# Last stage of a mixture-of-experts kernel: 71 tiles without a look-ahead behind them, rows of a partition side by side, first choices fetched early

## What is computed

```python
logits = flat @ gate_W.T                      # 4096 tokens, 8 experts
probs = softmax(logits); top_v, top_i = top_k(probs, 2)
g = silu(einsum('td,edf->etf', flat, w1_e))   # d=128, f=512
u = einsum('td,edf->etf', flat, w3_e)
out_e = einsum('etf,efd->etd', g * u, w2_e)
routed = einsum('te,etd->td', gates, out_e)
...
return 0.5 * shared + 0.5 * routed
x = x + gb * that                             # gb: one row of 128 per batch
```

## Time and profile before

| | us |
|---|---|
| median of 3 runs | 2277.46 (2275.94 to 2278.57) |
| profiled execution, its own time | 2262.21 |
| profiled execution, its span | 2260.4 |
| mean granted clock of TensorE in it | 0.987 |

### The profile page before, as it was taken

One profiled execution on the slowest core, in us unless ns is written; L12 is line 12 of the kernel. 1 busy time (PEld: TensorE's weight loads), 2 busy tenths in 40 slices (PEclk: granted clock), 3 DMA queues, 4 the chain that ended last, 5 costly groups with the idle time before them and its releaser, 6 DMA issues. The chain is left out here.

```text
span 2260.4 us, 40689 instructions
## 1 busy us (share of the span) xinstructions
PE 2172.6 (96%) x10606; PEld 1381.5 (61%) x10607; DVE 1811.6 (80%) x4826; ACT 1248.2 (55%) x1690; POOL 1385.5 (61%) x751
## 2 busy tenths in 40 slices
PE   7989999999999999999999999999999999989995
PEld 4756756556556565665656656565565654449884
DVE  7788887888888888888888888888888887765555
ACT  2333344566666666666666666666666663434442
POOL 2212121777777787787877777787777776643331
PEclk9999999999999999999999999999999999999997
DMA  7050220000001000000100000010000000411114
GB/s 251 26 201 1 87 80 31 24 17 13 16 18 33 17 13 16 18 14 16 31 16 18 16 14 13 16 36 17 14 13 18 17 8 11 153 43 49 47 45 138
DMA packets 90664, 91.79 MB, mean 41 GB/s; under 512 B 22261, under 2 KB 75125, under 8 KB 90553
## 3 DMA queue, kind: packets, MB, share of 16 engines
q1 hardware_dynamic: 86232, 81.88, 11.7%
q0 software_dynamic: 4352, 8.99, 1.2%
HBM read 57.90 MB, written 36.86 MB: 42 GB/s over the span
## 5 line engine op out<-in xcount | busy, mean ns | idle before, releaser
L1661 ACT ACTIVATE big<-P 128x1024 f32<-128x1024 f32 x512 | 512.6, 1021 | 99.6 <-PE P L2044 82.0
L2058 PE MATMUL P<-big,V 128*64 128x512 f32 x2048 | 470.5, 600 | 1.0 <-ACT big L1667 1.0
L658 POOL TENSOR_TENSOR spair<-spair,big 128x1024 f32<-128x1024 f32 x192 | 457.4, 2382 | 16.0 <-DVE hp L818 1.3
L658 POOL TENSOR_TENSOR opair<-opair,big 128x1024 f32<-128x1024 f32 x192 | 457.6, 2384 | 15.0
L1048 DVE CUSTOM_DVE_ANT_0 big<-P,near 128x512 f32<-128x512 f32 x512 | 349.0, 682 | 110.2 <-PE P L2028 107.7
L2028 PE MATMUL P<-kq 96*128 96x512 f32 x1008 | 414.2, 432 | 2.7 <-DVE kq L1036 1.4
L2043 PE MATMUL P<-kq 97*128 97x512 f32 x1024 | 409.5, 400 | 2.4 <-DVE xs L824 2.1
L1051 DVE TENSOR_REDUCE mhalf<-P 128x1 f32<-128x512 f32 x512 | 349.3, 682 | 76.7 <-PE P L2028 65.8
L2044 PE MATMUL P<-kq 128*128 128x512 f32 x1024 | 407.0, 397 | 0.0
L2028 PEld LDWEIGHTS P<-kq 96*128 96x128 f32 x1008 | 180.8, 189 | 204.1 <-issue 103.6
L2058 PEld LDWEIGHTS P<-big,V 128*64 128x64 f32 x2048 | 135.6, 137 | 266.3 <-issue 263.7
(11 more groups left out here) (333 smaller groups left out, 3636.2 us busy)
## 6 DMA issues: line engine op xcount, KB each, us to landing
slots<-later SPq DMA_DIRECT2D x4, 4224.0 KB, 16.1
kq<-auxrows SPq DMA_DIRECT2D x64, 128.0 KB, 2.2
wqk<-wparts SPq DMA_DIRECT2D x124, 64.0 KB, 1.8
big<-in_wex SPq DMA_DIRECT2D x8, 768.0 KB, 12.1
xt<-slots SPq DMA_DIRECT2D x76, 66.0 KB, 1.8
near<-in_aux SPq DMA_DIRECT2D x64, 64.0 KB, 1.8
big<-yrows SPq DMA_DIRECT2D x8, 512.0 KB, 7.2
xs<-in_x SPq DMA_DIRECT2D x4, 512.0 KB, 4.1
```

The source lines that it names most:

```text
L658: pool.tensor_tensor(psum8[s][:, :], psum8[s][:, :], pfull[:, j % RING, :], ALU.add).then_inc(S["p_added"], 1)
L1661: act.activation(pfull[:, j, :], banks(2 * (j % 2)), ACT.Exp, scale=DH1 ** -0.5).then_inc(S["exp_done"], 1)
L2058: mm = pe.matmul(P[64 * i:64 * i + 64, 4, :], V1[:, j, s, :], half(pfull[:, j, :], i), start=(j == 0), stop=(j == T - 1))
```

## The change

The number of steps becomes NT = 71, which is the most that can be filled (64 full tiles and 7 for the rounding). The loop now covers steps 24 to 47 alone, and steps 48 to 70 are written out on each engine, without the work for tiles that don't exist. The rows are renumbered: token p*8+t of a batch's numbering stands where t*128+p stood, so that a partition's eight rows lie side by side in `yrows` and are moved as one piece of 4 KB. The fetch is split: the four c = 0 transfers are issued as soon as the scatters of all tiles before the last expert's have landed (a count that DVE now works out in four operations more and puts at the end of `blk_i`, so that `S["map"]` goes to 4), the four c = 1 transfers at the end. DVE multiplies and adds c = 0 of batches 0 to 2 by themselves, ahead of c = 1; batch 3 is done as before. That is 15 operations on 128x1024 in place of 12.

```diff
+NT = K1N * NTOK // 128 + E1 - 1
+LAST = NSTEP // GROUP - 1
-    m[:, M_TOK:M_TOK + T] = 128 * np.arange(T) + i[:, None]
+    m[:, M_TOK:M_TOK + T] = np.arange(T) + T * i[:, None]
...
+        out_of = lambda i: 16 * len(range(i, NT, YBUF))
...
-            sp.wait_ge(S["map"], 2)
+            sp.wait_ge(S["map"], 4)
...
-            with sp.Fori(0, NSTEP // GROUP) as r:
+            with sp.Fori(0, LAST) as r:
...
+            for k in range(LAST * GROUP + XBUF, NT):
+                block = sp.value_load(blk_i[0:1, 0, k:k + 1], min_val=0, max_val=E1 * REGION)
+                sp.wait_ge(E["t_turned"], k - XBUF + 1)
+                sp.wait_ge(E["t_idx"], k - XBUF + 1)
+                load_tile(k, block)
+
+            def load_y(b, c):
+                rows = yrows[c * NTOK + b * N:c * NTOK + (b + 1) * N, :].rearrange("(p t) d -> p (t d)", p=128)
+                sp.dma_start(big[:, 2 * b + c, :], rows).then_inc(E[f"m_z_in{b}" if c else f"m_y_in{b}"], 16)
+
+            uptos = [sp.value_load(blk_i[0:1, 0, NBLK - 1 - i:NBLK - i], min_val=16 * NTOK // 128 // YBUF, max_val=out_of(YBUF - 1 if i else 0)) for i in range(2)]
             for i in range(YBUF):
-                sp.wait_ge(E[f"t_out{i}"], 16 * NSTEP // YBUF)
-            sp.wait_ge(E["t_down"], NSTEP)
+                sp.wait_ge(E[f"t_out{i}"], uptos[i // (YBUF - 1)])
             for b in range(B):
-                for c in range(K1N):
-                    rows = yrows[c * NTOK + b * N:c * NTOK + (b + 1) * N, :].rearrange("(t p) d -> p t d", p=128)
-                    sp.dma_start(tok(big[:, 2 * b + c, :]), rows).then_inc(E[f"m_y_in{b}"], 16)
+                load_y(b, 0)
+            for i in range(YBUF):
+                sp.wait_ge(E[f"t_out{i}"], out_of(i))
+            sp.wait_ge(E["t_down"], NT)
+            for b in range(B):
+                load_y(b, 1)
...
-                dve.tensor_scalar(blk_i[:, 0, :], block, float(E1 * REGION), None, ALU.min).then_inc(S["map"], 1)
+                dve.tensor_scalar(blk_i[:, 0, 0:NBLK - 2], block[:, 0:NBLK - 2], float(E1 * REGION), None, ALU.min).then_inc(S["map"], 1)
+                begun_at = ks[:, 0:NT:YBUF]
+                fills = later[:, 0:len(range(0, NT, YBUF)), 0]
+                step(dve.tensor_scalar(fills, begun_at, tiles_e[:, 2, E1 - 2:E1 - 1], 16.0, ALU.is_lt, ALU.mult))
+                stepped()
+                step(dve.tensor_reduce(tiles_e[:, 1, 0:1], fills, AX.X, ALU.add))
+                stepped()
+                for i, most in enumerate((out_of(0), out_of(YBUF - 1))):
+                    dve.tensor_scalar(blk_i[:, 0, NBLK - 1 - i:NBLK - i], tiles_e[:, 1, 0:1], float(most), None, ALU.min).then_inc(S["map"], 1)
...
-            with dve.Fori(1, NSTEP // GROUP) as r:
+            with dve.Fori(1, LAST) as r:
...
+            for j in range(GROUP):
+                left = NT - LAST * GROUP - j
+                if left > 3:
+                    tile_low(LAST, 3 + j, same)
+                if left > 1:
+                    tile_gu(LAST, 1 + j, same)
+                if left > 0:
+                    tile_out(LAST, j, same)
+                if left > 2:
+                    tile_dest(LAST, 2 + j, same)
+
+            AHEAD = 3
+            dve.wait_ge(E["m_x_in"], 16 * B)
+            for b in range(AHEAD):
+                ya, xb = tok(big[:, 2 * b, :]), tok(xs[:, b, :])
+                dve.wait_ge(E[f"m_y_in{b}"], 16)
                 dve.tensor_tensor(ya, ya, over(modb[:, b, :], tens), ALU.mult).then_inc(E["m_scaled"], 1)
                 dve.wait_ge(E["m_scaled"], b + 1)
-                xb = tok(xs[:, b, :])
-                dve.tensor_tensor(xb, xb, ya, ALU.add).then_inc(E["m_done"], 1)
+                dve.tensor_tensor(xb, xb, ya, ALU.add).then_inc(E["m_sum"], 1)
+            for b in range(B):
+                ya, yb, xb = tok(big[:, 2 * b, :]), tok(big[:, 2 * b + 1, :]), tok(xs[:, b, :])
+                dve.wait_ge(E[f"m_z_in{b}"], 16)
+                if b < AHEAD:
+                    dve.wait_ge(E["m_sum"], b + 1)
+                else:
+                    dve.wait_ge(E[f"m_y_in{b}"], 16)
+                    dve.tensor_tensor(yb, yb, ya, ALU.add).then_inc(E["m_sum"], 1)
+                    dve.wait_ge(E["m_sum"], b + 1)
+                dve.tensor_tensor(yb, yb, over(modb[:, b, :], tens), ALU.mult).then_inc(E["m_scaled"], 1)
+                dve.wait_ge(E["m_scaled"], AHEAD + b + 1)
+                dve.tensor_tensor(xb, xb, yb, ALU.add).then_inc(E["m_done"], 1)
...
+            es = experts_of(LAST * GROUP, GROUP)
+            for j in range(GROUP):
+                left = NT - LAST * GROUP - j
+                if left > 3:
+                    tile_turn(LAST, 3 + j, same)
+                if left > 2:
+                    tile_up(LAST, 2 + j, same, es[2 + j])
+                if left > 0:
+                    tile_down(LAST, j, same, es[j])
+                if left > 1:
+                    tile_gu_turn(LAST, 1 + j, same)
```

More of the change, by code:

```diff
@@ L203, in network @@
              "c_kept": S["ydT_copied"], "t_gate": S["gates"], "t_idx": S["dests"], "t_gu": S["gu_done"], "t_gu_turned": S["yd_turned"], "t_guT": S["hT_dve"],
-             "t_down": S["downd_mm"], "t_y": S["ydT_copied"], "m_x_in": S["mod_in"],
+             "t_down": S["downd_mm"], "t_y": S["ydT_copied"], "m_x_in": S["mod_in"], **{f"m_z_in{b}": S[n] for b, n in enumerate(("q0_mm", "k0_mm", "q0_min", "k0_min"))},
              "m_sum": S["x1_done"], "m_scaled": S["x1_scaled"], "m_done": S["x_ready"], "m_out": S["next_mod"]}
@@ L379, in end_batch @@
             e.sem_inc(G["passed"], 1)
+        assert XBUF == YBUF
+        out_of = lambda i: 16 * len(range(i, NT, YBUF))
         block = ctx.enter_context(nc.Block())
@@ L600, in _ @@
             for i in range(XBUF):
-                sp.wait_ge(G[f"t_in{i}"], 16 * (NSTEP + XBUF) // XBUF)
+                sp.wait_ge(G[f"t_in{i}"], out_of(i))
         @block.gpsimd
@@ L780, in _ @@
             end_batch(pool, -1)
-            with pool.Fori(0, NSTEP // GROUP) as r:
+            with pool.Fori(0, LAST) as r:
                 for j in range(GROUP):
@@ L787, in _ @@
                     pool.indirect_dma_start(yrows, bass.IndirectOffsetOnAxis(tidx[:, j % YBUF:j % YBUF + 1], 0), xn[:, j % YBUF, :], None).then_inc(E[f"t_out{j % YBUF}"], 16)
+            for k in range(LAST * GROUP, NT):
+                pool.wait_ge(E["t_y"], k + 1)
+                pool.indirect_dma_start(yrows, bass.IndirectOffsetOnAxis(tidx[:, k % YBUF:k % YBUF + 1], 0), xn[:, k % YBUF, :], None).then_inc(E[f"t_out{k % YBUF}"], 16)
         @block.vector
@@ L1893, in _ @@
                 tile_guT(0, 1 + j, same)
-            with act.Fori(1, NSTEP // GROUP) as r:
+            with act.Fori(1, LAST) as r:
                 for j in range(GROUP):
@@ L1898, in _ @@
                     tile_guT(r, 1 + j, act.snap)
+            for j in range(GROUP):
+                left = NT - LAST * GROUP - j
+                if left > 3:
+                    tile_T(LAST, 3 + j, same)
+                if left > 2:
+                    tile_silu(LAST, 2 + j, same)
+                if left > 1:
+                    tile_guT(LAST, 1 + j, same)
         @block.tensor
@@ L2516, in _ @@
                 tile_gu_turn(0, 1 + j, same)
-            with pe.Fori(1, NSTEP // GROUP) as r:
+            with pe.Fori(1, LAST) as r:
                 es = experts_of(r * GROUP, GROUP + 4)
```

## The result

| | before | after |
|---|---|---|
| median, us | 2277.46 (7 runs, 2275.94 to 2279.53) | 2268.61 (7 runs, 2262.71 to 2271.38) |
| profiled execution, its own time | 2262.21 | 2270.38 |
| its span | 2260.4 | 2268.5 |

The ratio is 0.996, 95% interval [0.995, 0.9969]: 8.9 us faster, between 7.1 and 11.4. The forecast was 2267.8.

A forecast was written before the change was run, and what follows sets the result against it. PE was taken to bound the stage until 2233, then waiting and elementwise work. Gains of 4.2 + 0.5 - 0.4 + 5.4 = 9.7 us off 2277.46 gave 2267.8, range 2264 to 2273.

The forecast's parts named there:

- Drain: Last steps: tile 71 gone, then without look-ahead each step a chain of 2.20 us; gains 4.2 us, bounds 3.4 to 4.25.
- Border: PE loading experts' numbers at tile 48: nearest to the first border, 2.05 above pitch; 0.5 us gained, bounds 1.5 gained, 0.5 lost.
- Contention: Scatters beside the early fetch land in 6.0 us instead of 2.3, delaying tiles 69 and 70; 0.4 us lost, bounds 0 to 1.0.
- Tail: Last copy to DVE's end: six operations under the hand-over, nine after; 24.26 us becomes 18.9, 5.4 gained.
- The map: Four more DVE operations, about 1 us, covered by SP's wait for POOL's drain; cost nothing, 1 us if uncovered.
- The leeway: Time from a scatter's start until it must have landed for the indices four tiles on: 4.9 us.
- longer-contention rival: Scatters 64 to 67 all at 6.0 us or more, drained steps late too; 2.5 us lost beyond the 0.4, 2270.3; chance 0.12.
- The rival in which it is locked out: DVE's six operations delay POOL's last scatter to 7.75 us behind the last copy; gain only 3.8, 2273.7; chance 0.05.
- rivals of the numbering: Rows 4 KB apart make scatters land late throughout the stage; at 6.0 us, 40 us more, about 2308; chance 0.03.
- the fetch that isn't early: c = 0 fetch starts only at the end; tail 1.3 us longer than before, 3.4 gained in all, 2274.1; chance 0.04.
- The clock's rival in the drain: TensorE's clock falls to 0.50 in the drained steps; two downs and turns take 2.4 us longer, 2270.2; chance 0.04.
- 15.3 us carried over: Medians lie 15.3 us above the profiled time for reasons the profile doesn't show; this difference was added to the forecast.

The follow-up runs named there:

- the four bursts: Changed kernel twice, with 512-byte pieces, and with nothing done ahead, all fetching four c = 0 batches at once: first down to last copy 204.06, 202.71, 203.11, 203.56 us.

## Why the prediction was right, and where its sizes were off

By the table the change took 9.7 to 12.3 us out of (b)+(c), three profiles of before against two of after; 0.3 to 0.7 went back ahead of the restart. The medians say 8.9 and 12.0 in two sessions. The predicted sum was 9.7. That the terms measured in the profiled execution, 3.9 + 1.4 - 1.5 + 5.9, give the same 9.7 is luck: border and tail were put 1.4 too low together, drain and contention 1.4 too high. What held is where the time goes: the drain as a chain, the tail by DVE's operations, contention on a single scatter. Term by term:

*Drain, 4.2 predicted, 3.9 measured.* The step without a turn took 2.72 as worked out (2.735). The two chained steps took 2.26 and 2.37 for 2.20, and down to copy 1.30 for 1.20: down itself takes 1.15 there instead of 1.05, behind a wait of 0.77 for ACT.

*Border, 0.5 predicted, 1.4 measured* against two profiles of before; 2.6 against the second, whose border was 6.19 and 3.40. There 1.0 of the excess is the clock, not the border: the same step of 5.17 in the first profile and of 6.19 in the second, as windows (columns as in the earlier trace rows), has 1.02 more of busy PE at a mean granted clock of 0.82. (The next step, 3.40 for 3.24, still falls into that stretch.)

```profile
2160.75:2165.92 5.17, 3.19 (x20) 2.64 (x19) 1.38 (x6) 1.39 (x4) 1.37 (x2) 1.00 0.19 53
```

```profile
2174.38:2180.57 6.19, 4.21 (x20) 3.36 (x19) 2.41 (x7) 1.57 (x4) 1.35 (x2) 0.82 0.16 46
```

What failed is to take the new border like the first one, 2.05 above the pitch: it is 1.74, against 2.75 before, which is 1.0. The first border itself takes 4.68 for 4.88, and the rest is single steps of 3.0 to 3.2 at other places. The upper bound of 1.5 held against two profiles of three.

*Contention, 0.4 predicted, 0.2 to 1.5 measured,* 0.8 as the mean of the four bursts. The step that failed in the profiled one is "at 6.0": landings reached 7.3. The leeway was also mis-sized, in the other direction. I had put 4.9 behind a scatter's start. From tile 48 on POOL starts a scatter 0.57 behind the copy, not 1.09 as in its loop, so 5.4 are left, and DVE's idle time adds 0.4 to 0.5. That gives 5.8 to 5.9, and it fits each row: landings of 5.4 to 5.8 cost 0 to 0.2, and 6.4, 6.8 and 7.3 cost 0.6, 1.0 and 1.5, what they exceed it by. Of the longer-contention rival the mechanism was real, one scatter and not four; its 2.5 beyond the 0.4 was too much.

*Tail, 5.4 predicted, 5.9 measured* (DVE ends at C + 18.41, before C + 24.26). DVE starts at C + 0.21 instead of C + 0.35 and takes 1.213 an operation instead of 1.235; the transfers do what was said. c = 1 is issued at C + 3.65 and its first batch is in use at C + 7.47 without a wait: 3.8 against the 3.6 taken, so that it landed just as DVE came to it. The C + 3.48 taken for the issue came near by two effects that nearly cancel: POOL starts the last scatter 0.5 sooner, which was not foreseen, and the scatter takes 0.7 longer, which was put at 0.6. The sentence that wide pieces do little held: 0.2 to 0.4.

*POOL's last scatter* was stretched from 0.96 to 1.69, at nothing, as taken. It is 1.68 or 1.69 in all eight profiles in which DVE's operations run beside it, and 0.96 in the six in which DVE waits then. The rival in which it is locked out did not come about. The Trainium skill ("SBUF — State Buffer", Who interferes with whom) has a DVE operation with two SBUF inputs and a GpSimd operation that reads SBUF contend for an exclusive lock; the trace shows one delay of 0.73 beside operations of 1.22, and POOL is not held for the whole row of six.

*The map, 0 predicted, 0.3 to 0.7 measured ahead of the restart.* This term failed by its cause. The earlier trace rows showed SP waiting for POOL, and I took POOL's end as given. Where POOL ends last, its last scatter is stretched by the shifted operations of DVE: 19.4 from the map's first operation to the restart, against 18.74 and 18.81 of before and 18.78 moved. In the other profiles POOL is one scatter further (its last begins 9.1 behind the map's first operation, not 10.4) and SP waits for TensorE: 17.73 to 18.05 against 17.39 of before. Moved, it is 17.45; there SP's wait is for POOL. These last two are one profile each. Both roads cost, and 1 us, the price named for a lost cover, bounds them.

*The rivals of the numbering and of the fetch that isn't early* are out by the steps of 2.835 and by SP's row at 2232.35. The clock's rival in the drain was not seen: in 2236.9:2247.1 of after, the drained steps, the granted clock is 1.00. At the first ups the clock does stand at 0.50 for a part, but not by the change: part (a) differs by 2.5 us between profiles of the kernel before, and after's 10.0 lies inside that range. The profiled pair owes it 0.6 of the stage's 10.3.

*15.3 us carried over* from a profile that lay that far below its median. That was right only because the difference lies outside the stage, which the prediction had not looked at: luck.

## What to carry to other kernels

Cut a stage out of both profiles by an event that both have before comparing spans; here the span grew by 8.1 us while the stage shrank by 10.3. A wait for one engine's drain covers work on another engine only if that work doesn't reach into the first one's last instruction. Fetching early the half of a result that is complete, and working on it under the last hand-over, was worth 5.4 us of tail, 2.9 of them by the work; the width of the pieces hardly counted, since DVE was the slower side. Neither of the two finer versions (fetches spaced, map moved) was shown to be faster as a time.

## What was unexpected

A scatter of one tile, mostly 2.2 to 2.5 us alone and at most 3.9 in the first profile of before, took 5.7 to 5.8 beside two 512 KB transfers and 5.1 to 7.3 beside four. Loads of numbers into PE's registers explain only 0.5 of the 1.74 us at a border, and spread over the steps they cost more, 0.08 a step. POOL started a scatter 0.57 us behind its copy where its code is written out and 1.09 in its loop. And the same code ran 15 us longer or shorter between 1920 and 2015 from one session and chip to another, with DVE's waits of 2 to 8 us; the cause is open.
